# A click-rate tower on one core: the end of the last super tile rearranged, and one-hots with immediates for the first two

## What is computed

```python
e = jnp.stack([tbl_f[ids[:, f]] for f in range(32)], axis=1)     # (2048, 32, 64)
gram = jnp.einsum('bnd,bmd->bnm', e, e)
z = gram[:, rows, cols]                                          # 496 pairs, rows < cols
h = jnp.concatenate([z, dense_ctx], axis=1)                      # (2048, 512)
h = jnp.maximum(h @ W_top1 + b_top1, 0.0)                        # 512 -> 512
h = jnp.maximum(h @ W_top2 + b_top2, 0.0)                        # 512 -> 256
y = h @ W_top3                                                   # 256 -> 1
```

## Time and profile before

| | us |
|---|---|
| median of three runs | 427.18 |
| profiled execution, its own time | 426.98 |
| its span | 425.2 |
| TensorE (PE) busy | 394.0 |
| VectorE (DVE) busy | 295.3 |
| POOL busy | 244.8 |
| ScalarE (ACT) busy | 168.9 |

### The profile page before, as it was taken

The page is one execution under the profiler, slowest core; times in us unless marked ns, Lnnn a source line. Parts: engine busy times, 40 slices in busy tenths (PEclk is TensorE's granted clock), DMA queues, the critical chain, the costliest instruction groups (busy, mean ns, idle before and its releaser), DMA issues.

```text
span 425.2 us, 14913 instructions
## 1 busy us (share of the span) xinstructions
PE 394.0 (93%) x5554; PEld 358.8 (84%) x5554; DVE 295.3 (69%) x1295; ACT 168.9 (40%) x323; POOL 244.8 (58%) x250
## 2 busy tenths in 40 slices
PE   1877878999999999999999999999999999996987
PEld 0665668998999899989999899989998999986865
DVE  0899999998998289856996389829985699211200
ACT  2766744533532254324532353225432453230212
POOL 4576786665665665655665666666656666552200
PEclk9999999999999999999999999999999999998999
DMA  4444615112241251123312241123212111220100
GB/s 108 142 140 157 214 23 112 39 25 43 57 123 29 65 103 48 24 56 58 105 26 47 54 120 23 32 63 80 68 22 64 35 20 25 50 47 13 39 15 1
DMA packets 21002, 26.72 MB, mean 63 GB/s; under 512 B 9542, under 2 KB 13862, under 8 KB 20051
## 3 DMA queue, kind: packets, MB, share of 16 engines
q1 hardware_dynamic: 12882, 17.62, 12.6%
q0 software_dynamic: 7872, 8.08, 12.3%
q10 hardware_dynamic: 176, 0.08, 0.1%
HBM read 21.46 MB, written 0.08 MB: 51 GB/s over the span
## 4 chain that ended last, share of the span: by engine, by line
POOLq 43%; issue 38%; POOL 10%; PE 4%; SPq 2%; DMA 1%; DVE 0%; ACT 0%; DVEq 0%
POOLq L270 43%; POOL rows L265 10%; PE mlp_ps L361 2%; SPq L206 1%; PE gram_ps L349 1%; PE mlp_ps L371 1%; DMA rows<-tbl,index 1%; SPq L237 0%; DMA pairs<-folded 0%; DMA pairs<-dense 0%; DVE folded L563 0%; ACT folded L466 0%; PE mlp_ps L378 0%; PE turn_ps L305 0%; DVE y_room L556 0%
## 5 line engine op out<-in xcount | busy, mean ns | idle before, releaser
L265 POOL DMA_INDIRECT rows<-tbl,index x240 | 241.6, 1007 | 146.0 <-issue 143.1
L578 DVE TENSOR_SCALAR onehot<-place,codes_sb 125x256 bf16<-125x256 f16 x1216 | 248.2, 294 | 8.5 <-PE turn_ps L332 5.2
L332 PE MATMUL turn_ps<-split_sb,onehot 125*128 125x192 bf16 x2432 | 219.3, 246 | 10.7 <-DVE split_sb L613 10.7
L332 PEld LDWEIGHTS turn_ps<-split_sb,onehot 125*128 125x128 bf16 x2432 | 200.0, 98 | 17.5 <-DVE split_sb L613 14.0
L473 ACT CAST parts<-turn_ps 128x384 bf16<-128x384 f32 x136 | 65.2, 479 | 127.0 <-PE turn_ps L332 126.3
L556 DVE COPY y_room<-mlp_ps 1x256 f32<-1x256 f32 x8 | 5.0, 627 | 78.6 <-PE mlp_ps L378 78.6
L361 PE MATMUL mlp_ps<-pairs,w_sb 128*128 128x256 f32 x256 | 56.9, 380 | 1.0 <-DMA pairs<-dense 1.0
L361 PEld LDWEIGHTS mlp_ps<-pairs,w_sb 128*128 128x128 f32 x256 | 48.0, 190 | 7.8 <-DMA pairs<-dense 1.6
L349 PE MATMUL gram_ps<-emb_t 64*64 64x64 f32 x2048 | 39.2, 226 | 0.9 <-DVE folded L563 0.5
L444 ACT COPY emb_t<-mlp_ps 128x512 f32<-128x512 f32 x58 | 34.0, 586 | 14.3 <-PE mlp_ps L302 13.6
L349 PEld LDWEIGHTS gram_ps<-emb_t 64*64 64x64 f32 x2048 | 34.8, 139 | 5.7 <-issue 5.7
(11 more groups left out here) (37 smaller groups left out, 124.3 us busy)
## 6 DMA issues: line engine op xcount, KB each, us to landing
place<-ids_scratch SPq DMA_DIRECT2D x6, 1062.5 KB
pairs<-folded SPq DMA_DIRECT2D x122, 32.0 KB
rows<-tbl,index POOLq DMA_INDIRECT x240
emb_t<-tbl SPq DMA_DIRECT2D x8, 250.0 KB
folded<-tbl SPq DMA_DIRECT2D x5, 312.5 KB
w_sb<-w SPq DMA_DIRECT2D x1, 1024.0 KB
y_room<-tbl SPq DMA_DIRECT2D x3, 312.5 KB
w_sb<-w SPq DMA_DIRECT2D x1, 512.0 KB
```

Source lines behind the costliest of these rows:

```text
L265: nc.gpsimd.indirect_dma_start(rows[:, s % 2, slot - UNITS, t, :], None, tables[f][:, :], bass.IndirectOffsetOnAxis(index[:, s, t, f:f + 1 ...
L332: last = nc.tensor.matmul(turn_ps[:, n % 2].rearrange("p k b -> p (k b)")[:, t * PARTS * DIM:(t + 1) * PARTS * DIM], onehot[:, n % RING, c ...
L578: last = nc.vector.tensor_scalar(onehot[:, n % RING, c, :], place[:, parity, u, :], codes_sb[:, CODE_AT[SPAN[u]] + c:CODE_AT[SPAN[u]] + c ...
```

## The change

Seven things change.

1. The ids of super tiles 0 and 1 are written to `place` less the first table row of their partition (an ACTIVATE with a bias from the new `shift_sb` in place of a copy). The one-hots of these two compare with an immediate, `float(c)`, in place of a column of `codes_sb`.
2. The pieces of ids are cut anew, so that the tables of one piece have the same size. SP loads `shift_sb` ahead of the tables.
3. Layer 1 of super tile 6 stands ahead of the last group of transposes of super tile 7, on TensorE and (its two halves of activations) on ScalarE. The 32 products on the identity are gone.
4. The transposes of super tile 7 use the two banks of `turn_ps` alone, since layer 1 writes the others.
5. Super tile 7's 16 moves are issued by three queues: SP 6, ACT 5, POOL 5.
6. Its dense features are loaded in the head into `last_dense` (five small DMAs on SP, with a mask), which VectorE clears first. When all moves have landed VectorE copies them into `pairs` under the mask, one COPY_PREDICATED of 128x1024. Layer 1 of super tile 7 waits for it.
7. Layers 2 and 3 of super tile 6 follow the Gram batches of super tile 7.

```diff
-PIECES = [(0, 4), (4, 8), (8, 12), (12, 16), (16, 17)]
+PIECES = [(0, 4), (4, 8), (8, 9), (9, 13), (13, 17)]
...
-SP_MOVES = 10
+SP_MOVES, ACT_MOVES = 6, 5
...
-                     for h in range(2)] + [turn_ps[:, 0], turn_ps[:, 1]]
+                     for h in range(2)]
+        last_bank = [turn_ps[:, 0], turn_ps[:, 1]]
...
+            sp.dma_start(shift_sb[:], shift).then_inc(shift_loaded, 16)
             sp.dma_start(codes_sb[:], codes).then_inc(codes_loaded, 16)
...
             sp.dma_start(second_sb[:], second).then_inc(second_loaded, 16)
+            sp.dma_start(dense_mask[:], dense_cells).then_inc(last_dense_loaded, 16)
+            sp.wait_ge(last_dense_cleared, 1)
+            for jj in range(CHUNKS):
+                sp.dma_start(last_dense[HALF + jj:P:FIELDS + CHUNKS],
+                             dense[SUPERS - 1].rearrange("(a b) (i q) -> b a i q", b=CHUNKS, i=QUAD)[jj]
+                             ).then_inc(last_dense_loaded, 16)
...
-            rearrange_pairs(SUPERS - 1, 1, own=SP_MOVES)
+            rearrange_pairs(SUPERS - 1, 1, own=SP_MOVES, place_dense=False)
...
-            for i, jq in MOVES[SP_MOVES:]:
+            for i, jq in MOVES[SP_MOVES + ACT_MOVES:]:
                 move_cells(pool, i, jq, 1).then_inc(moved_by_pool, 16)
...
                     if not ahead and g == GROUPS - 1:
+                        for o in range(OT1):
+                            layer1_tile(s - 1, o, 1 - parity, turn - 1 + parity)
                         pe.wait_ge(second_copied, GRAM_EMPTY + GRAM_BATCHES * s)
-                        stay_warm(WARM_LAST, last_warm)
-                    transpose_group(s, parity, turn, g, 2 if ahead else 4)
+                    transpose_group(s, parity, turn, g, turn_bank if ahead else last_bank)
...
-                nc.scalar.copy(place[:, s, a:b, :].rearrange("p u q -> p (u q)"),
-                               gram_flat[0:TP, piece % 2, 0:SUPER * (b - a)]).then_inc(placed, 1)
+                nc.scalar.activation(place[:, s, a:b, :].rearrange("p u q -> p (u q)"),
+                                     gram_flat[0:TP, piece % 2, 0:SUPER * (b - a)], ACT.Identity,
+                                     bias=shift_sb[:, piece:piece + 1]).then_inc(placed, 1)
...
             step(SUPERS - 1, 1, mlp=False, ahead=False)
-            for s in (SUPERS - 2, SUPERS - 1):
-                layer1_half(s, 0)
-                layer1_half(s, 1)
-                layer2_drain(s)
+            act.wait_ge(second_copied, GRAM_EMPTY + GRAM_BATCHES * SUPERS)
+            for i, jq in MOVES[SP_MOVES:SP_MOVES + ACT_MOVES]:
+                move_cells(act, i, jq, 1).then_inc(moved_by_act, 16)
+            layer2_drain(SUPERS - 2)
+            layer1_half(SUPERS - 1, 0)
+            layer1_half(SUPERS - 1, 1)
+            layer2_drain(SUPERS - 1)
...
                     last = nc.vector.tensor_scalar(onehot[:, n % RING, c, :], place[:, parity, u, :],
-                                                   codes_sb[:, CODE_AT[SPAN[u]] + c:CODE_AT[SPAN[u]] + c + 1], None, ALU.is_equal)
+                                                   codes_sb[:, CODE_AT[SPAN[u]] + c:CODE_AT[SPAN[u]] + c + 1]
+                                                   if s > 1 else float(c), None, ALU.is_equal)
...
+            dve.wait_ge(last_dense_loaded, 16 * (1 + CHUNKS))
+            dve.wait_ge(pairs_moved, 16 * (len(MOVES) * (SUPERS - 1) + SP_MOVES))
+            dve.wait_ge(moved_by_act, 16 * ACT_MOVES)
+            dve.wait_ge(moved_by_pool, 16 * (len(MOVES) - SP_MOVES - ACT_MOVES))
+            nc.vector.copy_predicated(pairs[:, 1].rearrange("p i j q -> p j i q"),
+                                      dense_mask[:].unsqueeze(2).unsqueeze(2).to_broadcast([P, CHUNKS, QUAD, QUADS]),
+                                      last_dense[:].unsqueeze(1).to_broadcast([P, CHUNKS, QUAD, QUADS])
+                                      ).then_inc(last_dense_placed, 1)
             layer3_drain(SUPERS - 2)
             layer3_drain(SUPERS - 1)
```

More of the change, by code:

```diff
@@ L44 @@
 RING = 4
-PIECES = [(0, 4), (4, 8), (8, 12), (12, 16), (16, 17)]
+PIECES = [(0, 4), (4, 8), (8, 9), (9, 13), (13, 17)]
 PIECE_OF = [p for p, (a, b) in enumerate(PIECES) for _ in range(a, b)]
-assert len(PIECE_OF) == UNITS == FIRST_UNITS
+assert len(PIECE_OF) == UNITS == FIRST_UNITS and all(len(set(SPAN[a:b])) == 1 for a, b in PIECES)
 SPANS = sorted(set(SPAN))
@@ L92, in slot_meaning, with build @@
     return rows, np.tile(second, (QUAD, SIDE))
-def build(nc, ids, tables, dense, w1, b1, w2, b2, w3, identity, second, looked_ids, codes, out):
+def build(nc, ids, tables, dense, w1, b1, w2, b2, w3, identity, second, dense_cells, looked_ids, codes, shift, out):
     fp32, i32, bf16, fp16 = mybir.dt.float32, mybir.dt.int32, mybir.dt.bfloat16, mybir.dt.float16
@@ L231, in rearrange_pairs @@
                     move_cells(sp, i, jq, parity).then_inc(pairs_moved, 16)
-                sp.wait_ge(pairs_moved, 16 * (len(MOVES) * s + own))
-                if own < len(MOVES):
-                    sp.wait_ge(moved_by_pool, 16 * (len(MOVES) - own))
+                if not place_dense:
+                    return
+                sp.wait_ge(pairs_moved, 16 * len(MOVES) * (s + 1))
                 for jj in range(CHUNKS):
@@ L355, in layer1_tile @@
             def layer1_tile(s, o, parity, turn):
-                if o == 0:
+                if o == 0 and turn is None:
+                    pe.wait_ge(last_dense_placed, 1)
+                elif o == 0:
                     pe.wait_ge(dense_placed[parity], 16 * CHUNKS * (turn + 1))
@@ L435, in _ @@
             step(SUPERS - 1, 1, SUPERS // 2 - 1, mlp=False, ahead=False)
-            for s in (SUPERS - 2, SUPERS - 1):
-                for o in range(OT1):
-                    layer1_tile(s, o, s % 2, s // 2)
-                layer2(s)
-                layer3(s)
+            layer2(SUPERS - 2)
+            layer3(SUPERS - 2)
+            for o in range(OT1):
+                layer1_tile(SUPERS - 1, o, 1, None)
+            layer2(SUPERS - 1)
+            layer3(SUPERS - 1)
         def drain_turned(engine, copy, done, s, g, banks):
@@ L444, in drain_turned @@
             copy(emb_t[:, :, GROUP_F * g:GROUP_F * (g + 1)],
-                 turn_bank[g % banks].rearrange("p f b -> p b f")).then_inc(done, 1)
+                 banks[g % 2].rearrange("p f b -> p b f")).then_inc(done, 1)
         def part(u, which):
@@ L492, in step @@
                             keep_parts(s + 1, u)
-                    drain_turned(act, nc.scalar.copy, turned_drained, s, g, 2 if ahead else 4)
+                    drain_turned(act, nc.scalar.copy, turned_drained, s, g, turn_bank if ahead else last_bank)
+                if not ahead:
+                    layer1_half(s - 1, 0)
+                    layer1_half(s - 1, 1)
                 for k in range(SLOTS):
@@ L661 @@
     second = given("second", second)
+    dense_cells = given("dense_cells", np.array([[p % FIELDS == HALF + CHUNKS * (p // FIELDS) + jj for jj in range(CHUNKS)]
+                                                 for p in range(P)]).astype(np.int32))
     looked_ids = given("looked_ids", x["ids"][:, LOOKED_UP].reshape(SUPERS, SUPER, UNITS).transpose(0, 2, 1)
                        .reshape(P, UNITS * BATCH // P))
+    shift = given("shift", np.stack([-SPAN[a] * np.arange(TP) for a, _ in PIECES], axis=1).astype(np.float32))
     codes = given("codes", np.concatenate([span * np.arange(TP)[:, None] + np.arange(span) for span in SPANS], axis=1)
@@ L667 @@
     out = nc.dram_tensor("out", (BATCH, 1), mybir.dt.float32, kind="ExternalOutput").ap()
-    build(nc, ids, tables, dense, w1, b1, w2, b2, w3, identity, second, looked_ids, codes, out)
+    build(nc, ids, tables, dense, w1, b1, w2, b2, w3, identity, second, dense_cells, looked_ids, codes, shift, out)
     return run_bass_kernel_spmd(nc, [arrays], core_ids=[0]).results[0]["out"]
```

29 lines of the change are left out of this document (19 added, 10 removed).

## The result

The changed kernel takes **440.72 us** (median of six runs, 436.89 to 443.12) against 427.24 for the kernel before beside it: ratio 1.0306, 95% interval 1.025 to 1.0362. It is 13.5 us slower, where 4.5 us faster was forecast. The profiled execution took 441.31, its span 439.5, which is 14.3 more than before.

The account below looks back on a forecast made before the run. POOL's gathers, then a 35.7 us path, were taken to bound the kernel. The new end gave -5.2 (last layer 1 at 405.3, not 410.5), the clock +0.7: -4.5, so 422.7 us, range 420.5 to 425.4.

Parts of the forecast that it names:

- The step that failed: POOL's row of gathers: 240, none waiting for another engine where followed; super tile 7's last fields arrive at 389.5 regardless of TensorE.
- the last 0.04 of the chances: The rest: some delay of the gathers or the head that eats most of the gain; chance 0.04.
- The slower case of my rivals: TensorE's clock stays at the lower level from 389.5 to the end: +10.7 us, 437.9; chance 0.05.
- Immediates: Head one-hots: 0 to 1.57 us gained per field; TensorE reaches super tile 7 0 to 5.6 earlier, 5.6 taken; end unaffected.
- Layer 1 of super tile 6 moved up: Before the last transposes: hidden if the head gains 5.6 us; with no gain it ends 0.9 after the gathers' landing.
- the first fall of the clock: In super tile 7's Grams, costing 1.1 us before; stays with the head's gain, goes without it; 0 taken.
- The moves: Super tile 7's 16 moves on SP, ACT and POOL: done at 403.9 against 406.4, ACT's landing taken as 1.88.
- the masked copy: VectorE's dense copy replaces four DMAs and their landing (4.07 us): 1.3 taken, bounds 0.72 and 1.44, plus 0.1 wait.
- the rival of the late ACT queue: ACT's fifth move lands at 406.5, not 403.9: +2.6, giving 424.6, or 425.3 with the clock's share; chance 0.10.
- The clock once more: TensorE's idleness around layer 3 of super tile 6 may slow the last layer 1: 0 to 1.7 us, +0.7 taken.
- Last gather "within a us or so of 387.1": Sign to check: POOL's last gather still issued near 387.1; the prediction is wrong if it moves.

Follow-up runs that it names:

- e6: Kernel before with the changed kernel's head alone (immediates, shifted ids, new pieces, the shift's load), old end, on a chip of ordinary speed: 442.18 us, ratio 1.0353.
- e13: Changed kernel, but the first of each field's 8 or 10 head one-hots reads its zero by pointer; ordinary-speed chip: 424.79 us, ratio 0.9945.
- e5: Changed kernel with its head put back (pointers, plain copies, old pieces), so the new end alone; ordinary-speed chip: 423.85 us, ratio 0.9926.
- e14: New end alone, old head, plus 12 and 14 products on the identity around layer 3 of super tile 6; ordinary-speed chip: 422.49 us, ratio 0.9901.
- e7: Changed kernel with VectorE in the head waiting for its own last one-hot after every field; ordinary-speed chip: 424.18 us, ratio 0.9918.
- e2: Kernel before with the changed kernel's head alone, old end, on the chip where the kernel before takes 540.77: 557.0 us, ratio 1.0304.
- e9: Changed kernel with VectorE's self-wait in the head after every fourth field only, on the chip where the kernel before takes 581.71: 588.49 us, one run.
- e1: Changed kernel with its head put back, so the new end alone, on the chip where the kernel before takes 540.77: 541.49 us, ratio 1.0013.
- e11: New end alone, old head, plus 12 and 14 identity products around layer 3 of super tile 6, on the 582 us chip: 582.75 us, ratio 1.0028.

## Why the prediction was wrong, point by point

- **The step that failed** is in the first paragraph: 240 gathers, "and none waits for another engine in the stretches that I followed", with "Whatever TensorE does, super tile 7's last four fields arrive at 389.5". I asked what TensorE does to the gathers and never what VectorE does. The rows were there: gathers of the head that take up to 2.11 us where 0.94 is usual, begun in a two-input subtraction. I had bounded what the immediates gain ("It does not matter which for the end") and put their price at zero, looking only at the copies of the ids and at the loads. The runs showed a price on another engine: one gather held for 31.7 to 36.5 us, and the last one issued 13.3 (e6) to 16.7 us late (the changed kernel). A delay of the gathers stood in my forecast only in the last 0.04 of the chances, without a size. The slower case of my rivals was about the clock; that its 437.9 lies near the 440.7 that came is chance.
- A small slip of the same paragraph: 240 gathers from 2.87 to 387.10 are 239 steps, 1.61 us each, not 1.59. Nothing rests on it.
- The rule that I overlooked stands in the Trainium skill, "SBUF — State Buffer", section "Who interferes with whom": VectorE and GpSimd share a pair of ports as an exclusive lock, which tensor_scalar in its two-port modes takes for the whole instruction, and which GpSimd's writing of descriptors needs (this last the page calls inferred). The traces agree that one-hots with immediates hold a gather, and go beyond it: the block lasted 31.7, 34.8 and 36.5 us, over 147 to 169 instructions back to back. No run here shows the ports themselves, nor in which mode a one-hot runs.
- *Immediates*: 135.5 ns each, 196 before; TensorE's first transposes came 6.1 us earlier. In e13 it begins layer 1 of super tile 6 at 379.19, in e5 at 383.10: 3.9 us of it are left there, inside the bounds of 0 and 5.6, where I had taken 5.6. That gain is worth little for the end, as said.
- *Layer 1 of super tile 6 moved up*: 7.07 us, no loss where it stands; in e5, where nothing is gained in the head, it starts at 383.10, and the transposes follow at 390.01, some 0.3 us past the landing (387.33 + 2.42), and in e14 1.1 past it, for which 0.9 was put down; the first fall of the clock stays away in both. Right.
- *The moves*: six on SP in 4.07, the fifth on ACT issued within 3.13, landing 2.2 after the issue (1.88 taken, 5.1 as the far end); *the masked copy* 1.30 for 1.3. Together -4.9 for -5.2. Right; the rival of the late ACT queue falls.
- *The clock once more*: +0.7 taken, 1.7 as the most, +1.4 (e5) to +3.0 (e13) measured. Mis-sized, since I let a fall last one stretch of 3.5; in three of four traces (the changed kernel, e7, e13) it lasted two. Here the rule of the Trainium skill, "TensorE: Matmul & The Clock Gate", section on the HAM clock gate, that an idle array is put back to 1.2 GHz, was the better guide than the one row with 1.00 that I set against it. With the block gone and the 2.8 of e7 in its place the sum becomes -4.9 + 2.8 = -2.1, which is 427.2 - 2.1 = 425.1: e7 and e13 measured 424.2 and 424.8. So even with the long gather gone the change would have come in above the 422.7 of the forecast, inside its range.
- Last gather "within a us or so of 387.1" was named as the point where the prediction would be wrong if it moved. It moved by 16.7, so the sign that I had named for a wrong prediction is the one that showed.

## What to carry to other kernels

When an instruction of VectorE is made faster in its form (here an immediate for a pointer; other forms were not tried), look at what POOL does beside it, above all at indirect DMAs that it issues: its gathers had slack only as long as VectorE's stream had openings. A stretch of VectorE without idle time is where to look, and a longest instruction per engine beside the mean is what to ask for; a mean of 1126 in place of 1007 ns hid one of 34.80 us. One comparison by pointer, or a pause of 0.03 us, per 2.8 us of such a stream was all that it took.

## What the runs showed of the hardware that was not expected

- One gather on POOL can be held for 31.7 to 36.5 us by VectorE instructions of 0.14 to 0.8 us that follow each other without a pause; it ended about 0.82 us after VectorE stopped (63.07 to 63.89 in the changed kernel, 62.75 to 63.57 in e2, 62.55 to 63.36 in e6), as if nearly all of its 0.94 were still to do. The two shorter blocks of e9 ended 0.82 after (50.37 to 51.19) and 0.12 after (74.64 to 74.76), the second as if only its end had been held. A block of over 30 us came in each of the three profiled executions that had immediates and neither pointer nor self-wait in the head, and in none of the others; the six times of the changed kernel, all from 436.89 up, are of its size. What separates the gather that is caught from those ahead of it that pass in 0.94 to 1.56 stays open.
- After the block of the changed kernel POOL starts a gather every 1.25 us, not 1.57, for 60 gathers, and regains 17 of 34 us. Why the gap goes back from 0.30 to 0.62 while it is still 16.7 us behind was not tried.
- Two chips took 541 and 582 us for the kernel that takes 427 on the others. The new end is worth nothing there (ratios 1.0013 for e1 and 1.0028 for e11), where TensorE and not the gathers bounds it (80% and 75% of their chains that ended last are TensorE). Why TensorE is slower on them was not looked into.
